# A state-space convolution and a LoRA MLP on one core: 64-row taps' operands from shifted images in DRAM, and the next tile's x parts ahead of the first tile's gating

## The reference

```
x = x + conv_layer(x, length, ...)   # causal convolution over 512 positions, 32 heads
x = x + mlp_layer(x, ...)            # 512 -> 1376 (gate, up) -> 512, LoRA per batch row

conv_layer:  K = 2 * Re(sum_n Cs[h,n] * exp(dtA[h,n] * l))        # 512 taps for each head
             y = (K convolved with masked u) + D * u, masked by length
mlp_layer:   gate = x Wg^T + 0.5 * (x A_g^T) B_g^T ;  up likewise  # A, B by adapter of the batch row
             act  = silu(gate) * up
             down = act Wd^T + 0.5 * (act A_d^T) B_d^T
```

## Time and profile before

| | |
|---|---|
| median of the runs | 540.23 us |
| the profiled execution | 540.83 us, of it span 538.8 us |
| mean granted clock of TensorE | 0.987 |
| TensorE matmuls busy | 494.6 us (92% of the span) |
| VectorE, ScalarE, GpSimd busy | 243.8, 153.1, 38.8 us |
| moved by DMA | 82.79 MB, mean 154 GB/s |
| `toep` loads | 16 of 512 KB, median 7.5 us from issue to landing |
| `um` loads | 16 of 256 KB, median 5.4 us |

### The profile page before, as it was taken

One profiled execution on the slowest core, in us unless ns is written; L12 is line 12 of the kernel. 1 busy time (PEld: TensorE's weight loads), 2 busy tenths in 40 slices (PEclk: granted clock), 3 DMA queues, 4 the chain that ended last, 5 costly groups with the idle time before them and its releaser, 6 DMA issues.

```text
span 538.8 us, 9538 instructions
## 1 busy us (share of the span) xinstructions
PE 494.6 (92%) x3036; PEld 443.0 (82%) x3036; DVE 243.8 (45%) x489; ACT 153.1 (28%) x283; POOL 38.8 (7%) x55
## 2 busy tenths in 40 slices
PE   0098798599999999999999999999999999999997
PEld 0087697588898989898988889898989898989896
DVE  7883164454343535353535344444435353534423
ACT  5781002422322222222322231322222222222221
POOL 1006700000000000000000000000000000000000
PEclk9999799989999999999999999999999999999999
DMA  7899995274748484949474747475757665665601
GB/s 261 301 328 375 297 325 155 40 156 97 149 105 153 116 152 117 152 116 154 112 155 118 154 113 153 118 143 119 140 127 140 127 139 133 131 143 112 151 31 39
DMA packets 182614, 82.79 MB, mean 154 GB/s; under 512 B 128034, under 2 KB 165474, under 8 KB 182594
## 3 DMA queue, kind: packets, MB, share of 16 engines
q1 hardware_dynamic: 182594, 82.54, 64.0%
HBM read 63.46 MB, written 19.04 MB: 153 GB/s over the span
## 4 chain that ended last, share of the span: by engine, by line
PE 84%; DMA 5%; DVE 5%; SPq 3%; issue 1%; ACT 0%; DVEq 0%; ACTq 0%
PE ps_g L1113 16%; PE ps_u L1113 16%; PE ps_da L1045 13%; PE ps_db L1045 12%; PE ps_x L1113 11%; PE ps_g L1081 5%; PE ps_g L1008 3%; DMA toep<-kpad 3%; PE ps_x L1037 2%; DMA kpad<-k_sb 2%; PE ps_u L1008 2%; PE ps_u L1045 2%; PE ps_x L1081 1%; PE ps_da L1072 1%; SPq L366 1%
## 5 line engine op out<-in xcount | busy, mean ns | idle before, releaser
L886 DVE TENSOR_TENSOR ht_lo<-h_raw,ht_hi 128x512 fp32r<-128x512 f32 (+1 forms) x45 | 27.1, 603 | 92.0 <-ACT ht_hi L537 80.7
L537 ACT CAST ht_hi<-h_raw 128x512 fp32r<-128x512 f32 (+1 forms) x45 | 24.7, 549 | 154.7 <-DMA h_raw<-hrow 150.3
L1113 PE MATMUL ps_g<-w_hi,x_hi 128*128 128x512 f32 x128 | 51.8, 405 | 7.2 <-DVE x_lo L843 5.8
L907 DVE TENSOR_TENSOR h_act<-h_act,ps_u 128x512 f32<-128x512 f32 x32 | 22.0, 688 | 73.5 <-ACT h_act L572 73.5
L1113 PE MATMUL ps_u<-w_hi,x_hi 128*128 128x512 f32 x128 | 51.7, 404 | 0.0
L1113 PE MATMUL ps_g<-w_lo,x_hi 128*128 128x512 f32 x128 | 51.5, 402 | 0.0
L1113 PE MATMUL ps_g<-w_hi,x_lo 128*128 128x512 f32 x128 | 51.4, 402 | 0.0
L1113 PE MATMUL ps_u<-w_hi,x_lo 128*128 128x512 f32 x128 | 50.6, 396 | 0.0
L1113 PE MATMUL ps_u<-w_lo,x_hi 128*128 128x512 f32 x128 | 50.5, 395 | 0.0
L1045 PE MATMUL ps_da<-wd_hi,ht_hi 128*128 128x288 f32 (+1 forms) x165 | 50.4, 306 | 0.0
L1045 PE MATMUL ps_db<-wd_hi,ht_lo 128*128 128x288 f32 (+1 forms) x165 | 48.7, 295 | 0.0
(11 more groups left out here) (214 smaller groups left out, 1073.1 us busy)
## 6 DMA issues: line engine op xcount, KB each, us to landing
b_raw<-btab SPq DMA_DIRECT2D x128, 86.0 KB, 2.8
toep<-kpad SPq DMA_DIRECT2D x16, 512.0 KB, 7.5
h_raw<-hrow SPq DMA_DIRECT2D x30, 256.0 KB, 3.2
ad_raw<-dtab SPq DMA_DIRECT2D x64, 88.0 KB, 2.4
um<-xr SPq DMA_DIRECT2D x16, 256.0 KB, 5.4
x<-xT SPq DMA_DIRECT2D x8, 512.0 KB, 7.7
w_raw<-wgu SPq DMA_DIRECT2D x8, 512.0 KB, 10.5
a_raw<-atab SPq DMA_DIRECT2D x64, 64.0 KB, 1.9
```

Source lines behind the costliest of these rows:

```text
L537: nc.scalar.copy(ht_hi[:, f0:f0 + full, :], raw[:, 0:full, :]).then_inc(hthi_ok, 1)
L886: V.tensor_tensor(ht_lo[:, f0:f0 + full, :], raw[:, 0:full, :], ht_hi[:, f0:f0 + full, :].bitcast(F32), ALU.subtract).then_inc(htlo_ok, 1)
L907: V.tensor_tensor(h_act[:, 0:w], h_act[:, 0:w], ps_up[c][:, 0:w], ALU.mult).then_inc(act_ok, 1)
L1113: T.matmul(ps[:, 0:w], xs[:, kb, :], ws[:, kb, col:col + w], start=(kb == 0 and xs is x_hi and ws is w_hi), stop=False)
```

## The change

The taps of a pair are held in 128 partitions as 64 rows for each of the two heads, 576 columns wide, and a convolution makes twice as many matmuls of 64 rows; the two heads lie on the two halves of the partitions and write two PSUM banks. For pairs 0 to 3 the slot is loaded straight from `kpad` by two DMAs of 64 partitions. For groups 1 to 3, `copy_taps(g)` first writes eight images of each head's taps, shifted by eight elements from one to the next, to the new DRAM tensor `krep`, and one DMA of 128 partitions reads a pair from there. There are six `toep` slots, five `um` slots and three PSUM buffers of two banks. SP's order in the first stage is rewritten, and on VectorE `taps(1)` stands ahead of `phases(3)`. In the body of tile 0 (k == 0), ScalarE's and VectorE's parts of the next x stand ahead of the gatings of tile 0. `xr` is laid out on the host for the 64-row order. The diff, without a few repeated lines:

```diff
@@ -39,6 +39,14 @@
 DA_W = 288
 DB_W = NL - DA_W
 RC = 4
+RT = 6
+RU = 5
+RP = 3
+HR = P // 2
+HW = NL + HR
+NCP = 8
+ROWS = HR // NCP
+CW = HW + ROWS
 PAIRS = NH // 2
 PA, PB = 32, 16
 HG = 8
@@ -71,6 +79,7 @@
         xrow = nc.dram_tensor("xrow", (2 * P, NL), F32, kind="Internal")
         hrow = nc.dram_tensor("hrow", (FB * P, P), F32, kind="Internal")
         kpad = nc.dram_tensor("kpad", (NH, P + NL), F32, kind="Internal")
+        krep = nc.dram_tensor("krep", (NH * NCP, CW), F32, kind="Internal")
         w_hi = sb(top, "w_hi", [P, KB, WG], F32R)
@@ -124,8 +133,8 @@
         with ExitStack() as pa:
             with ExitStack() as pz:
                 zeros = sb(pz, "zeros", [NH, P])
-            toep = sb(pa, "toep", [P, RC, 2, NL])
-            um = sb(pa, "um", [P, RC, 2 * KB * NB])
+            toep = sb(pa, "toep", [P, RT, HW])
+            um = sb(pa, "um", [P, RU, 2 * KB * NB])
             lmask = sb(pa, "lmask", [P, KB, NB], I32)
             k_sb = sb(pa, "k_sb", [PA, NG, HG, PB])
@@ -146,16 +155,14 @@
         ht_lo = sb(top, "ht_lo", [P, FB, P], F32R)
-        ps_g = [top.enter_context(nc.psum_tensor(f"ps_g{i}", [P, 512], F32)) for i in range(2)]
-        ps_u = [top.enter_context(nc.psum_tensor(f"ps_u{i}", [P, 512], F32)) for i in range(2)]
+        ps_c = [top.enter_context(nc.psum_tensor(name, [P, 2, 512], F32)) for name in ("ps_gg", "ps_uu", "ps_xx")]
+        ps_g, ps_u, ps_x = ([both[:, i, :] for i in range(2)] for both in ps_c)
         ps_da = top.enter_context(nc.psum_tensor("ps_da", [P, 512], F32))
         ps_db = top.enter_context(nc.psum_tensor("ps_db", [P, 512], F32))
-        ps_x = [top.enter_context(nc.psum_tensor(f"ps_x{i}", [P, 512], F32)) for i in range(2)]
         ps_k = [ps_da, ps_db]
         ps_gate = [ps_g[0], ps_g[1], ps_x[0]]
         ps_up = [ps_u[0], ps_u[1], ps_x[1]]
         ps_turn = [ps_g[0], ps_g[1], ps_x[1]]
-        ps_c = [ps_g[0], ps_g[1], ps_u[0], ps_u[1]]
         prm_in, len_in, idx_in = sem("prm_in"), sem("len_in"), sem("idx_in")
@@ -169,8 +176,9 @@
         ang_in, ang_out, tab_ready = sem("ang_in"), sem("ang_out"), sem("tab_ready")
         k_ps, k_ready, zero_out = sem("k_ps"), sem("k_ready"), sem("zero_out")
         k_out = [sem(f"k_out{g}") for g in range(NG)]
-        toep_in = [sem(f"toep_in{i}") for i in range(RC)]
-        um_in = [sem(f"um_in{i}") for i in range(RC)]
+        k_rep = [sem(f"k_rep{g}") for g in range(NG)]
+        toep_in = [sem(f"toep_in{i}") for i in range(RT)]
+        um_in = [sem(f"um_in{i}") for i in range(RU)]
         conv_ps, x1_ok = sem("conv_ps"), sem("x1_ok")
         x0_hi, x0_lo, x0_sel = sem("x0_hi"), sem("x0_lo"), sem("x0_sel")
@@ -230,9 +238,18 @@
             return bass.AP(tensor=kpad, offset=g * HG * (P + NL) + P, ap=[[PB, PA], [P + NL, HG], [1, PB]])
-        def shifted_taps(pair):
-            return bass.AP(tensor=kpad, offset=pair * (2 * (P + NL)) + 1, ap=[[1, P], [P + NL, 2], [1, NL]])
+        def direct_taps(pair, h):
+            return bass.AP(tensor=kpad, offset=(2 * pair + h) * (P + NL) + 1, ap=[[1, HR], [1, HW]])
+        def copied_taps(pair):
+            return bass.AP(tensor=krep, offset=2 * pair * NCP * CW, ap=[[CW, 2 * NCP], [1, ROWS], [1, HW]])
+        def toep_need(pair):
+            direct = RC > pair % RT
+            return 16 * (pair // RT + 1) + (16 if direct else 0)
         block = top.enter_context(nc.Block())
@@ -252,16 +269,28 @@
                 sp.wait_ge(k_ready, g + 1)
                 sp.dma_start(taps_rows(g), k_sb[:, g, :, :]).then_inc(k_out[g], 16)
-            def load_toep(pair, slot, group):
-                sp.wait_ge(k_out[group], 16)
-                wait(sp, conv_ps, pair - RC + 1)
-                sp.dma_start(toep[:, slot, :, :], shifted_taps(pair)).then_inc(toep_in[slot], 16)
-            def load_um(pair, slot, first):
-                if not first:
-                    sp.wait_ge(conv_ps, pair - RC + 1)
-                sp.dma_start(um[:, slot, :], xr[bass.ds(pair * P, P), :]).then_inc(um_in[slot], 16)
+            def copy_taps(g):
+                sp.wait_ge(k_out[g], 16)
+                from_ = bass.AP(tensor=kpad, offset=g * HG * (P + NL) + 1, ap=[[P + NL, HG], [ROWS, NCP], [1, CW - 1]])
+                into = bass.AP(tensor=krep, offset=g * HG * NCP * CW, ap=[[NCP * CW, HG], [CW, NCP], [1, CW - 1]])
+                sp.dma_start(into, from_).then_inc(k_rep[g], 16)
+            def load_toep(pair):
+                slot, g = pair % RT, pair // RC
+                if g == 0:
+                    sp.wait_ge(k_out[0], 16)
+                    for h in range(2):
+                        sp.dma_start(toep[h * HR:(h + 1) * HR, slot, :], direct_taps(pair, h)).then_inc(toep_in[slot], 16)
+                else:
+                    sp.wait_ge(k_rep[g], 16)
+                    wait(sp, conv_ps, pair - RT + 1)
+                    sp.dma_start(toep[:, slot, :], copied_taps(pair)).then_inc(toep_in[slot], 16)
+            def load_um(pair):
+                wait(sp, conv_ps, pair - RU + 1)
+                sp.dma_start(um[:, pair % RU, :], xr[pair * P:(pair + 1) * P, :]).then_inc(um_in[pair % RU], 16)
             def indices(a, q):
@@ -286,7 +315,7 @@
             sp.wait_ge(consts, 1)
             sp.dma_start(kpad.ap()[:, 0:P], zeros[:, :]).then_inc(zero_out, 16)
             for pair in range(RC):
-                load_um(pair, pair, True)
+                load_um(pair)
             load_x(0, 0)
             load_x(0, 1)
             for n in range(2 * KB):
@@ -295,23 +324,37 @@
             ids0 = indices(0, 0)
             sp.wait_ge(zero_out, 16)
             store_taps(0)
+            for pair in range(RC):
+                load_toep(pair)
             load_piece(2 * KB)
-            for pair in range(RC):
-                load_toep(pair, pair, 0)
-            for n in range(2 * KB + 1, NP_GU):
-                load_piece(n)
+            load_piece(2 * KB + 1)
             load_x(1, 0)
+            for pair in range(RC, RU):
+                load_um(pair)
             store_taps(1)
             load_x(1, 1)
             load_x(2, 0)
-            for pair in range(RC, 2 * RC):
-                load_um(pair, pair - RC, False)
-                load_toep(pair, pair - RC, 1)
-                if pair == RC:
-                    load_x(2, 1)
-                if pair >= RC + 2:
-                    store_taps(pair - RC)
-                    load_x(3, pair - RC - 2)
+            copy_taps(1)
+            for pair in range(RU, 2 * RC - 1):
+                load_um(pair)
+            load_toep(RC)
+            load_um(2 * RC - 1)
+            load_toep(RC + 1)
+            load_toep(RC + 2)
+            load_x(2, 1)
+            store_taps(2)
+            load_toep(RC + 3)
+            load_um(2 * RC)
+            copy_taps(2)
+            store_taps(3)
+            load_x(3, 0)
+            copy_taps(3)
+            load_toep(2 * RC)
+            load_um(2 * RC + 1)
+            load_toep(2 * RC + 1)
+            load_piece(2 * KB + 2)
+            load_x(3, 1)
+            load_piece(2 * KB + 3)
             def load_b(t, ids):
                 wait(sp, u_ps, NC * t)
@@ -342,12 +385,12 @@
                 sp.wait_ge(y_ok, 2 * t + 2)
                 sp.dma_start(out[bass.ds(t * P, P), :], y_sb[:, :]).then_inc(y_out, 16)
-            for pair in range(2 * RC, PAIRS):
-                load_um(pair, pair % RC, False)
-                load_toep(pair, pair % RC, pair // RC)
-                if pair == 2 * RC:
+            for pair in range(2 * RC + 2, PAIRS):
+                load_um(pair)
+                load_toep(pair)
+                if pair == 2 * RC + 2:
                     load_a(0, ids0)
-                if pair == 2 * RC + 1:
+                if pair == 2 * RC + 3:
                     sp.wait_ge(mask_done, KB + 1)
                     load_b(0, ids0)
             for n in range(NP_GU, len(pieces)):
@@ -583,11 +626,13 @@
                         top_part(n)
                 act.wait_ge(tm_ok, t + 1)
                 nc.scalar.copy(t_hi[:, :], t_m[:, :, :].rearrange("p h b -> p (h b)")).then_inc(thi_ok, 1)
+                if k == 0:
+                    x_hi_part(t + 1)
                 for c in range(NC):
                     silu(c)
                     if last:
                         turned_hi_part(c)
-                if not last:
+                if k > 0 and not last:
                     x_hi_part(t + 1)
                 if k == 0:
                     for n in range(NP_GU + 3, NP_GU + 6):
@@ -795,7 +840,7 @@
                 dve.wait_ge(x_in[2 * pair // HG], 32)
                 V.copy_predicated(x[:, 2 * pair:2 * pair + 2, :, :].rearrange("p h k b -> p h (k b)"),
                                   lmask[:, :, :].rearrange("p k b -> p (k b)").unsqueeze(1).broadcast_to([P, 2, KB * NB]),
-                                  ps_c[pair % RC][:, :].rearrange("p (h n) -> p h n", h=2)).then_inc(x1_ok, 1)
```

(36 more changed lines are left out.)

## The result

The changed kernel takes 551.29 us (median of 4, 547.77 to 552.17) beside 539.79 (539.28 to 541.24) for the kernel before: ratio 1.020, interval 1.016 to 1.024. It is about 11 us slower; 536.5 was predicted, with 541.5 as the upper end. A few executions, told by a lower clock or a time far above the rest, fell in a slower state of the chip and are left out of all medians. The profiled execution's span is 549.2 us against 538.8.

What follows compares the result with a forecast made beforehand. The prediction took the DMA queue to bound the first stage up to 61 us, TensorE after it, and SP's queue from tile 0 to tile 1. Loads -6.7 and x parts +3.0 gave -3.7: 536.5 us, range 532.3 to 541.5.

Steps and rivals of the forecast that it cites:

- The matmuls: TensorE's convolutions: the two row halves run side by side, 2.41 us a pair; bounds 2.41 and 4.82.
- rival 2: TensorE from 25.5 on: halves do not run side by side in fp32, about +5 to +18 us; chance 0.13.
- conv(0) at 25.5: First stage: smaller tap loads land earlier, so the first convolution starts 2.5 us earlier, at about 25.5.
- conv(4) at 41.8: First stage: taps(3) on TensorE ends near 41.8 and conv(4) starts there instead of at about 44.
- at 392 GB/s: DMA queue up to pair 12: 2.5 MB less to move, at 392 GB/s worth 6.5 us of queue time.
- The hops: Taps' store and copy through DRAM: pair 4 lands at 40.9, just in time, pair 8 near 51.3.
- the 3 to 4 us: Sign on the copies: the prediction is wrong if they land later than 3 to 4 us after issue.
- The clock: TensorE at conv(12): a hole of 1.9 us may lower the clock; half of 2.55 taken, 1.3 us.
- x parts: +3.0: Tile 0 to tile 1: x parts moved ahead delay t_m by 0.55, slow clock adds 2.4; bounds +0.55 and +3.5.
- Sum: Whole kernel: -6.7 from the loads and +3.0 from the x parts give -3.7 us.
- Rival 3: First stage: copy waits and b_raw hold conv(12) to 66 or later, clock drops; -3.5 + 3.5, 540.2 us; chance 0.14.
- only in the first fifth: Kernel before: clock slices read as full from about 130 us to the end, lowered only in the first fifth.

Runs made afterwards that it cites:

- plain_no_hops: Changed kernel with x parts behind the gatings, no copies, every pair loaded by one DMA of 128 plain rows of x: 534.81 us, ratio 0.990.
- plain_grouped: plain_source with its 128 rows read as sixteen groups of eight, 64 bytes between groups: 545.76 us, ratio 1.015.
- plain_source: Changed kernel without the x parts' move, its twelve loads from krep replaced by plain rows of x, copies kept: 540.89 us, ratio 1.003.
- t_only: Kernel before, with t's and then b's operations ahead of the parts of h in tile 1: 542.52 us, ratio 1.006.
- one_load: Changed kernel with x parts behind the gatings, no copies, each pair loaded from kpad in one DMA, two heads outermost: 616.34 us, ratio 1.142.
- plain_halves: plain_no_hops with each pair loaded by two DMAs of 64 partitions: 541.19 us, ratio 1.002.

## Why the prediction was wrong, point by point

- **The matmuls** (2.41 a pair, rival 2 the only danger): right, 2.40. The side on which the forecast looked for a slowdown was sound.
- **conv(0) at 25.5, conv(4) at 41.8 if its taps are there**: right as to TensorE and VectorE (25.60; TensorE is free for `conv(4)` at 40.75 in the changed kernel and begins it at 42.28 in plain_no_hops).
- **"at 392 GB/s"**: the first step that failed. The rate was carried over from loads of the kernel before to loads of another shape. With `um` between them, those of sixteen groups of eight run at 253 to 265 in a full queue, those of 64 partitions at 250 to 258. The saved 2.5 MB, worth 6.5 us of queue, are used up by that alone: with hops kept, plain rows instead of grouped ones are worth 4.9 to 6.6 us (plain_grouped against plain_source, medians and ratios). The prediction read the Trainium skill's rule on half the ports and applied it to pairs 0 to 3 only, where it is hidden; of the full-width load's form it asked nothing.
- **The hops** (store in 2.2 to 3.6 us, copy "just in time", SP stopped for about a microsecond): the second. Stores took 5.45 and 6.34, pair 4 came 2.8 us late (43.7 for 40.9), pair 8 7.2 late (58.5 for 51.3) and `conv(12)` began at 76.1 for 64. The lag grows because group 2's store is issued behind group 1's loads (43.20 for 41.0), takes 2.7 us longer than assumed, and group 3's store (3.00) has to land too before SP issues pair 8. The first copy kept to the 3 to 4 us that the prediction named as a sign (3.66); the stores did not. The prediction started from the 1.7 us of a store that met an empty queue. But the kernel before has a store behind a backlog too, that of group 2, and it is the longest DMA piece in its chain that ended last, up to the first tile:

```profile
40.32 9.15 DMA kpad<-k_sb
```

The prediction assumed 3.6 us for it; with what this line shows it would have put pair 8 later than 51.3. Price of the hops: 540.9 (plain_source) less 534.8 (plain_no_hops), 6.1 us, in which pairs 0 to 3 in halves are contained.

- **The clock** (one hole, 1.3 us): too small. Late taps make three longer holes, and the convolutions behind them lose about 6 us, where the kernel before lost about 3. This follows from the two steps above and is no cause of its own. Also, the price that the prediction took from `conv(9)`, 4.96 - 2.41 = 2.55, compares a busy time with a distance between starts; by starts it is 66.15 - 61.41 - 2.41 = 2.33.
- **x parts: +3.0** measured 3.6 by the ratio. The wait for SP's chain and the slow clock behind it were right in kind (6.63 us, at half clock behind it; about 9 predicted); left out was the table load of 1.28 us, which had lain in idle time between `t_hi` and the first silu and comes behind `x_hi` once that stands between.
- **Sum**: -6.7 and +3.0 forecast; measured alone +7.3 and +3.0 by the medians, +6.7 and +3.6 by the ratios. Rival 3 (queue gain used up) named both mechanisms, stores landing late and SP's stops, and was priced at the `conv(12)` of 66; it was right in kind and 10 us short. Either of the two losses of the loads alone leaves their part at about no gain (540.9, 541.2), as rival 3 had it; both together were not among the cases.
- **A reading:** the clock is not lowered "only in the first fifth" before; the ninth of the forty slices (108 to 121 us) is lowered too.

What stays open: how the rows of a grouped source are dealt out to the engines (the rate and the longer packets were seen), how the price of the hops divides between their own time and SP's stops, and why t_only is slower.

## What to carry to other kernels

A byte count divided by the trace's GB/s is a price only for loads of the same shape: before halving a transfer, ask how the new one is written (outermost dimension, partitions reached), and if no row shows that form, let the range hold a rate a third lower. A hop through DRAM in the middle of a saturated queue waits its turn behind the backlog, here once each for store, copy and load, and a 16 KB store is no exception (5.45 and 6.34 us). Its time is to be taken from a row under the same load and not from one alone. And where an operation is moved ahead of another kind on ScalarE, count the table load that moves with it; where a wait is removed, see first which later wait in program order has no slack.

## What the runs showed of the hardware

- Loads of 128 rows of 2304 bytes, with `um` between them, run in a full queue at 389 GB/s when the rows are one dimension of 128 and at 259 when they are sixteen groups of eight (plain_source, plain_grouped); a row takes 93 and 136 ns (medians). With two heads outermost the queue moves 51 GB/s at a share of 0.13 (one_load).
- In two DMAs of 64 partitions the same rows come at 258 GB/s where full width has 387 (plain_halves, plain_no_hops).
- Row starts moved by 4 bytes cost nothing (540.11 and 540.89 us, 93 ns a row in both).
- fp32 matmuls of 64 rows on the two halves run fully side by side, two passes each: 2.40 us for 32 of them.
- Issuing a 64-partition load of taps takes SP 0.62 us (5.00 for eight) where 0.48 was taken from loads of full width.
